# Projections as three fp16 products, values copied by ScalarE, rows normalised by GpSimd, in an attention and experts kernel

## The reference

```
x = x + attention(layernorm(x))      # 16 heads of 16, causal; qkv = xn @ W_qkv + b_qkv; out @ W_out + b_out
x = x + experts(layernorm(x))        # 8 experts, top 2 per token, h = gelu(xn @ w1 + b1), out = h @ w2 + b2
```

## Time and profile before

| | |
|---|---|
| median of 3 runs | 950.83 us (948.45 to 956.42) |
| the profiled execution | 945.29 us, span of its records 943.5 us |
| mean granted TensorE clock | 0.931 of 2.4 GHz |
| busy: PE, DVE, ACT, POOL | 89%, 74%, 61%, 49% |
| chain that ended last, by engine | PE 52%, DVE 17%, DMA 14%, SPq 7%, issue 4% |

### The profile page before, as it was taken

How to read it: one execution, slowest core, us unless ns; L and a number is a source line. 1 busy time by engine, 2 the same in 40 slices (tenths; PEclk the granted TensorE clock), 3 DMA queues, 4 the chain that set the end, 5 groups by cost and what they waited for, 6 DMA issues and landing times.

```text
span 943.5 us, 21008 instructions
## 1 busy us (share of the span) xinstructions
PE 835.8 (89%) x6760; PEld 553.9 (59%) x6760; DVE 697.6 (74%) x1566; ACT 572.8 (61%) x1048; POOL 465.0 (49%) x575
## 2 busy tenths in 40 slices
PE   4899987877888979888898699998999999999996
PEld 3555422332243525333343589887888888888875
DVE  6777888868659798898986487884686766566664
ACT  2777466656758787877978374563544554455453
POOL 4200032323535665757486647784567564555441
PEclk9999988888887888889897899999999999999999
DMA  9888767754666868567855965445535554544341
GB/s 208 269 278 263 247 179 231 208 143 145 192 182 189 202 169 215 152 195 188 210 118 146 251 115 110 75 85 99 80 53 100 81 77 63 87 77 78 58 70 24
DMA packets 185047, 139.40 MB, mean 148 GB/s; under 512 B 98064, under 2 KB 167568, under 8 KB 184816
## 3 DMA queue, kind: packets, MB, share of 16 engines
q1 hardware_dynamic: 153444, 95.16, 39.7%
q0 software_dynamic: 15776, 18.95, 13.1%
q10 hardware_dynamic: 15724, 23.95, 7.9%
HBM read 83.63 MB, written 44.80 MB: 136 GB/s over the span
## 4 chain that ended last, share of the span: by engine, by line
PE 52%; DVE 17%; DMA 14%; SPq 7%; issue 4%; POOL 2%; ACT 1%; POOLq 0%; ACTq 0%; DVEq 0%
PE banks L777 17%; PE banks L795 17%; PE banks L599 5%; DVE arena L1240 3%; PE banks L716 3%; DMA arena<-inverse_sums 2%; DMA weighed_values<-arena 2%; SPq L1818 2%; PE banks L702 2%; DVE weights L1402 2%; PE banks L589 2%; SPq L1816 2%; DVE arena L1242 2%; DMA arena<-token_rows,arena 2%; DVE arena L1237 2%
## 5 line engine op out<-in xcount | busy, mean ns | idle before, releaser
L996 ACT ACTIVATE arena<-banks,arena 128x256 f32<-128x256 f32 (+1 forms) x312 | 152.8, 542 | 187.1 <-PE banks L777 96.2
L777 PE MATMUL banks<-arena,weights 128*128 128x256 f16 (+1 forms) x1872 | 205.3, 266 | 12.3 <-DMA arena<-arena 11.7
L777 PEld LDWEIGHTS banks<-arena,weights 128*128 x1872 | 174.7, 98 | 38.0 <-issue 14.4
L795 PE MATMUL banks<-weights,arena 128*128 x1704 | 193.8, 273 | 0.8 <-DVE arena L1532 0.8
L1739 POOL DMA_INDIRECT out<-arena x71 | 116.0, 1634 | 141.4 <-DVE arena L1543 89.8
L795 PEld LDWEIGHTS banks<-weights,arena 128*128 128x128 f16 x1704 | 165.2, 98 | 22.3 <-issue 1.7
L658 PE MATMUL banks<-arena 64*128 64x128 f16 (+3 forms) x512 | 121.4, 334 | 19.4 <-ACT arena L907 6.9
L1530 DVE TENSOR_SCALAR arena<-arena 128x512 f16<-128x512 f32 (+1 forms) x156 | 75.3, 483 | 74.8 <-ACT arena L996 73.2
L630 PE MATMUL banks<-arena 62*128 62x384 f16 (+3 forms) x512 | 95.7, 330 | 34.3 <-DVE arena L1237 11.6
L1532 DVE SCALAR_TENSOR_TENSOR arena<-arena 128x512 f16<-128x512 f32 (+1 forms) x156 | 110.1, 706 | 5.5
L658 PEld LDWEIGHTS banks<-arena 64*128 64x128 f16 x512 | 38.4, 100 | 105.4 <-issue 34.4
(11 more groups left out here) (199 smaller groups left out, 1283.1 us busy)
## 6 DMA issues: line engine op xcount, KB each, us to landing
weights<-in_L_ffn_w ACTq DMA_DIRECT2D x16, 1024.0 KB, 8.3
arena<-in_L_ffn_w SPq DMA_DIRECT2D x32, 512.0 KB, 4.9
qk_parts<-weights SPq DMA_DIRECT2D x64, 128.0 KB
arena<-qk_parts SPq DMA_DIRECT2D x128, 64.0 KB, 3.5
weighed_values<-arena SPq DMA_DIRECT2D x32, 256.0 KB
token_rows<-arena SPq DMA_DIRECT2D x12, 512.0 KB, 4.2
arena<-qk_parts SPq DMA_DIRECT2D x128, 32.0 KB, 3.7
arena<-weighed_values SPq DMA_DIRECT2D x32, 128.0 KB
```

The lines of the kernel that those rows point to most:

```text
L777: m = pe.matmul(bank[:, c * TILE:c * TILE + WIDTH[j]], w1[:, k, wp, f:f + P], xp[:, k, 0:WIDTH[j]], start=(i == 0), stop=(i == len(terms) ...
L795: m = pe.matmul(bank[:, c * D:(c + 1) * D], hp[:, f, c * P:(c + 1) * P], w2[:, f // (FC // 2), wp, f % (FC // 2), :], start=(f == 0 and i ...
L996: m = act.activation(h_32[r % 2][:, c, 0:WIDTH[j]], banks[:, 1 + c2, c * TILE:c * TILE + WIDTH[j]], ACT.Gelu, bias=b1_now[j % 2][:, 2 * c2 ...
```

## The change

- **TensorE.** Batch 0 stays in fp32. In batches 1 to 7 each fp32 product becomes three fp16 products (high by high, high by low, low by high) of parts of the rows and of the weights. The order within a batch becomes values 0, c = 0, values 1, c = 1, transposes, c = 2, c = 3. After batch 1 two small products make `b_v @ W_out` (`value_bias`).
- **ScalarE.** The transposed rows are copied as an fp16 part, scaled by 16; the values are copied here (`copy_v`), without a bias; the full fp32 copies of query and key go for batches 1 to 7. It makes the fp16 part of W_qkv once (three instructions of 512 columns) and no longer normalises batches 2 to 7.
- **VectorE.** It makes the low parts of the rows (two per batch, `low_rows`) and of W_qkv (three once) and those of query and key straight from PSUM. The bias of the values is added to the output bias once. `know_rows` takes single batches from batch 3 on, and eight of its small steps are replaced by one power on GpSimd, for which it waits. `qk_scales_2` comes ahead of `know_rows(1)`. Magnitudes: one matrix in each of batches 2, 3, 4 and 6; two matrices more are left to attention, where loads and magnitudes stand 30 ticks apart rather than 36.
- **GpSimd.** The roots (`row_roots`), the columns of W_v in another order (two copies), the memset of `rows`, and the normalising of batches 2 to 7 (four instructions of 256 columns each). The split of the output bias comes in batch 2.
- **SyncE.** b1 goes to tick 132 of attention, the eleven DMAs of the empty rows to ticks 60 to 260, the search for the expert scales and the first weight splits some 12 to 18 ticks later.

```diff
-            at(i * 36 + 30, "load_weights", i + EARLY)
-            at(i * 36 + 92, "magnitude", (i + EARLY, 0))
-            at(i * 36 + 110, "magnitude", (i + EARLY, 1))
+            at(i * 30 + 30, "load_weights", i + EARLY)
+            at(i * 30 + 92, "magnitude", (i + EARLY, 0))
+            at(i * 30 + 110, "magnitude", (i + EARLY, 1))
...
+        for i in range(B - PARTS[0][0] + 2):
+            at(60 + 40 * i, "spare", i)
+        at(132, "b1", 0)
+        at(384, "find_scales", 0)
...
-        together = [[0]] + [list(range(b, min(b + 2, B))) for b in range(1, B, 2)]
+        together = [[0], [1, 2]] + [[b] for b in range(3, B)]
...
+                    w.wait_ge(sem("w_in_low"), 1)
+                    w.wait_ge(sem("x_low"), 2 * b)
+                    terms = [(k, w_in[:, wp], x_parts[b % 2][:, xp]) for k in range(KC)
+                             for xp, wp in ((0, 0), (0, 1), (1, 0))]
...
-                for half in range(2):
-                    for s in range(2):
-                        tt = half * 2 + s
-                        for k in range(KC):
-                            m = pe.matmul(banks[:, (4, 7)[half], s * D:(s + 1) * D],
-                                          x_T[b % 2][:, k, tt * P:(tt + 1) * P], w_qkv[:, k, 2 * D:3 * D],
-                                          start=(k == 0), stop=(k == KC - 1))
...
+                    if c < 2:
+                        for s in range(2):
+                            tt = c * 2 + s
+                            for i, (k, w_, x_) in enumerate(terms):
+                                m = pe.matmul(banks[:, (4, 7)[c], s * D:(s + 1) * D], x_[:, k, tt * P:(tt + 1) * P],
+                                              w_v[:, k, :] if b == 0 else w_[:, k, 2 * D:3 * D], start=(i == 0), stop=(i == last))
+                        m.then_inc(sem("v_made"), 1)
                     number = 2 * KC * b + c
                     bank = banks[:, 5 + c % 2, :]
                     if number >= 2:
-                        w.wait_ge(sem("qk_full"), number - 1)
-                    for k in range(KC):
-                        m = pe.matmul(bank, w_qkv[:, k, c * P:(c + 1) * P], x_T[b % 2][:, k, :],
-                                      start=(k == 0), stop=(k == KC - 1))
+                        w.wait_ge(sem("qk_low"), number - 1)
+                    for i, (k, w_, x_) in enumerate(terms):
+                        m = pe.matmul(bank, w_[:, k, c * P:(c + 1) * P], x_[:, k, :], start=(i == 0), stop=(i == last))
                     m.then_inc(sem("qk_made"), 1)
...
+            def value_bias():
+
+                w.wait_ge(sem("vectors_in"), 80)
+                for k in range(KC):
+                    m = pe.matmul(banks[:, 3, 0:D], b_v[:, k:k + 1].broadcast_to([P, P]), w_out[:, k, :],
+                                  start=(k == 0), stop=(k == KC - 1))
+                m.then_inc(sem("value_bias"), 1)
...
+                    else:
+
+                        act.activation(qk_part[b % 2][c][:, 0, :], banks[:, 5 + c % 2, :], ACT.Identity,
+                                       bias=b_qk[:, c:c + 1], scale=1.0).then_inc(sem("qk_high"), 1)
...
+                w.wait_ge(sem("roots_known"), i + 1)
+                for step in range(2, 5):
                     m = own.mark(rsqrt_step(step, variance_, inverse, rest))
                     yield
...
+            def low_rows(b):
+                for k in range(KC):
+                    w.wait_ge(sem("xT"), 2 * b + k + 1)
+                    v.scalar_tensor_tensor(x_parts[b % 2][:, 1, k, :], banks[:, (4, 7)[k], :], ROWS_UP,
+                                           x_parts[b % 2][:, 0, k, :], ALU.mult, ALU.subtract).then_inc(sem("x_low"), 1)
...
+                    else:
+                        w.wait_ge(sem("qk_high"), number - 2 * KC + 1)
+                        v.scalar_tensor_tensor(low, banks[:, 5 + c % 2, :], b_qk[:, c:c + 1], qk_part[b % 2][c][:, 0, :],
+                                               ALU.add, ALU.subtract).then_inc(sem("qk_low"), 1)
+                    if c == 1 and b + 1 < B:
+                        low_rows(b + 1)
                     if b >= OPEN and opening[2 * KC * (b - OPEN) + c]:
                         maxima(*opening[2 * KC * (b - OPEN) + c])
-                    w.wait_ge(sem("qk_full"), number + 1)
-                    both(qk_part[b % 2][c][:, 1, :], qk_full[number % 2], qk_part[b % 2][c][:, 0, :], ALU.subtract).then_inc(
-                        sem("qk_low"), 1)
+                    for _ in range(4):
+                        next(following, None)
+                    if c % 2 == 1 and b in MAGNITUDES_IN:
+                        magnitude(MAGNITUDES_IN.index(b), (c // 2,))
...
+            qk_scales_2()
             for _ in know_rows(1):
...
+            def row_roots(i):
+                n = TT * len(together[i])
+                w.wait_ge(sem("sums_known"), i + 1)
+                g.tensor_tensor(newton_1[i % 2][1][:, 0:n], newton_1[i % 2][0][:, 0:n],
+                                minus_half.rearrange("p n t -> p (n t)")[:, 0:n], ALU.pow).then_inc(sem("roots_known"), 1)
+
+            row_roots(0)
+            w.wait_ge(sem("w_qkv_in"), 32)
+            for k in range(KC):
+                g.tensor_copy(w_v[:, k, :].rearrange("p (g d h) -> p g h d", g=NG, h=HG),
+                              w_qkv[:, k, 2 * D:3 * D].rearrange("p (g h d) -> p g h d", g=NG, h=HG)).then_inc(
+                    sem("w_v_turned"), 1)
             w.wait_ge(sem("qk_own"), 1)
             g.partition_all_reduce(Q_ALL, Q_OWN, P, bass.bass_isa.ReduceOp.max).then_inc(sem("qk_all"), 1)
             g.memset(v_blocks[1][:, :, HG * HD:V_WIDE], 1.0)
             for s in range(4):
                 g.memset(q_st[s], 0.0)
                 m = g.memset(k_st[s], float(2 ** SHIFT))
+                if s == 1:
+                    row_roots(1)
...
+            def normalise(b):
+                i = group_of[b]
+                col = TT * together[i].index(b)
+                w.wait_ge(sem("rows_known"), i + 1)
+                w.wait_ge(sem("normed"), b)
+                w.wait_ge(sem("x_turned"), 2 * (b - 2) + 2)
+                for tt in range(TT):
+                    m = g.tensor_scalar(x_norm[b % 2][:, tt, :], x_in[b % 4][:, tt, :],
+                                        newton_1[i % 2][1][:, col + tt:col + tt + 1],
+                                        newton_1[i % 2][3][:, col + tt:col + tt + 1], ALU.mult, ALU.add)
+                m.then_inc(sem("normed"), 1)
...
+            for b in range(1, B):
+                if b + 1 < B:
+                    normalise(b + 1)
+                if b + 2 < B:
+                    row_roots(group_of[b + 2])
+                if b == 2:
+                    split_bias()
+                if b == B - 2:
+                    top_split(0)
...
-            for b in range(PARTS[0][0], B):
-                sp.dma_start(rows_dram[b * T:(b + 1) * T, 0:D].rearrange("(t p) d -> p t d", p=P), rows).then_inc(
-                    sem("spare_rows"), 16)
-                sp.dma_start(rows_dram[b * T:(b + 1) * T, D:ROW].rearrange("(t p) e -> p t e", p=P),
-                             rows[:, :, 0:E]).then_inc(sem("spare_rows"), 16)
...
+                elif stage == "spare":
+                    lay_spare(n)
+                elif stage == "b1":
+                    sp.dma_start(b1_sb, t["L0_ffn_b1"].rearrange("e (c p) -> p e c", p=P),
+                                 allow_slow_non_contiguous=True).then_inc(sem("b1_in"), 16)
```

224 lines of the change are left out of this document (137 added, 87 removed).

## The result

The changed kernel took **960.49 us** (median of 9 runs, 957.56 to 966.66) against 950.83 us (9 runs of the kernel before beside it, 939.97 to 966.98). The ratio is **1.0141, 95% interval 1.0106 to 1.0175**: slower. The forecast was 949 us with 936 to 963, and its likeliest case, no change, did not come; the rival of 962 us came nearest. The profiled execution took 960.49 us, its span 958.6 us.

A forecast was written before the change was run, and what follows sets the result against it. TensorE was taken to bound the projections and VectorE early attention. Projections -14.5, start +7.2 and attention +5.2 summed to -2.1 us; with the 5.5 us offset of the median carried over, 949 us, range 936 to 963.

The forecast's parts named there:

- the rival of 962 us: Early attention: SyncE stands behind b1's load up to 15.4 us instead of 2, giving 962 us; chance 0.15.
- four signs: Wrong if: first fp16 product before 32 us, batches near 9, SyncE issue over 5 near unit 6, projections clock below 0.95.
- The products: TensorE in the projections: fp16 products take a batch from 11.2 to 8.8 us, 2.4 us less.
- The pace of VectorE: Projections: VectorE needs 10.0 us in batches 2 to 4, above TensorE's 8.8; seven batches 73.8 us, 14.5 us gained.
- The start: Before batch 1: its fp16 products start at 38.0 us where they were at 30.78, 7.2 us lost.
- two changes of code: GpSimd at the start: changing code before the reduction and before the power of 8 columns, up to 7.3 us each.
- The first rival: Start: GpSimd's changes of code are off the path, batch 1 at 28.3 to 31 us, 939 to 942 us; chance 0.23.
- Attention: Early attention: magnitudes 2.2 us, b1 2 us and empty rows 1 us, together about 5 us lost.
- SyncE stands behind b1: Attention, tick 132: b1's 2.20 + 13.19 us recur, shifting the load of unit 6 and later ones; 962 us, chance 0.15.
- the third rival: TensorE's clock falls to a mean of 0.86 through waits at the start and in each batch; 955 us, chance 0.12.
- The empty rows: SyncE in attention: two issues of 0.43 us at five places, mostly in gaps, cost 1 us (bounds 0 and 9).
- The magnitudes: VectorE in attention: two matrices more, four magnitudes of 1.12 us, half counted, 2.2 us lost (bounds 0 and 4.8).

The follow-up runs named there:

- bias_split_late: The changed kernel with the split of the output bias on GpSimd in batch 6 in place of batch 2; 959.91 us, ratio 1.0139 to the kernel before.
- b1_back: The changed kernel with only the load of b1 back at the start of SyncE's queue; 950.01 us, ratio 0.9976 to the kernel before.
- reduction_first: The changed kernel with roots of batches 0 to 2 on VectorE and GpSimd's reduction ahead of its two copies; 977.25 us, ratio 1.0062 to the kernel before.
- roots_on_vector: The changed kernel with roots of batches 0 to 2 back on VectorE in eleven small steps; 963.77 us, ratio 1.0106 to the kernel before.

## Why the prediction was wrong

**What bounds the kernel: right.** TensorE was the bound of the projections, and work moved into attention met another bound. But I read attention's bound as VectorE's busy share alone. The queue that feeds both engines was in the account only for b1 and the empty rows, at 3 us in all. Three of the four signs that I had named for being wrong came: batches near 9 us, a SyncE issue of over 5 us near the load of unit 6, and a granted clock below 0.95 in the projections.

**The products: right. The pace of VectorE: too slow.** 12 fp16 products of 256 columns and 6 of 512 take about 1.3 us, as the 1.32 that I took; `low` and `low_rows` came near the 0.65 us taken. Batches 2 and 4 took 8.67 us each, which is TensorE's 8.8; I had put 10.1 on the strength of VectorE's 10.0, and VectorE was busy for only 6.2 and 7.0 us of them. Batch 3 took 15.0 us for 10.1, with the 3.85 us of batch 4's late rows and 1.7 us more for the twelve products behind them. Batches 1 to 7 took from 38.91 to 115.3 us, 76.4 us against 73.8, so that the sum is near in part because these two misses have opposite signs. GpSimd's normalising was counted at nothing with the sentence that the transposes would wait if it were late; the split of the output bias and its three DMA issues, 59.70 to 64.69 us, stood right ahead of it and were not put into that sum.

**The start: both idles came, the size in part by luck.** Forecast 38.0, measured 38.91. The sum has two changes of code at 7.3 us each. No run shows that GpSimd changes its code there; the traces have idles of 6.73 and 7.00 us that nothing in the profile ends, at the two places. ScalarE had batch 1 normalised at 31.88 us, 1.1 ahead of the sum. From there I had put 5.0 us and it took 7.0: TensorE had waited 7.49 us, the granted clock was 0.62 from 33.50 to 38.50 us, and eight fp32 products, 3.60 us in the kernel before at 1.00, took 5.37:

```profile
33.70 5.37 PE L623 MATMUL banks<-weights 128*128 128x512 f32 x8
```

The place given for the idle of the reduction was too narrow: it also came with only the two copies ahead, at 8.41 us, and not where the reduction stands first, behind its wait for VectorE (7.49 us). That before it was hidden in such a wait, as the sum has it, no trace shows. And the sum had no memset that holds VectorE (in the kernel before one tensor_scalar was held for 1.24 us at 17.61, a row that I had passed over); in the changed kernel that hold hid behind the second idle, and it took its price only when the powers were gone. The first rival, with this time off the path and batch 1 at 28.3 to 31 us, did not come true.

**Attention: this step failed.** "I take 2 us on the path: issue within the gap, part of the rest on the load (bounds 0 and 15.4)". The issue did fill the gap, with 2.45 us, and then nothing of the gap was left (0.1 us): the next issue stood for 10.37 us, and with b1 back at the start units 1 and 2 were 8.3 us closer, unit 2 came 10.6 us earlier, and the ratio fell by 0.0165, some 16 us with wide bounds. The rival SyncE stands behind b1 had the place, the mechanism and the time, 962 us against 960.49, and I gave it 0.15. Against it I had put that other loads filled the engines at the start; in attention they were nearly as full: the DMA share was 1.16 from 9.19 to 22.38 us in the kernel before, and 1.09 from 147.50 to 158.00 us in the changed one. The rows at hand give a sum of that size: the load that waits has no slack but SyncE's gap of 4.2 us, and 2.20 + 13.19 less that gap is 11.2. But this is no proof of a rule: in the kernel before, where that gap was read, b1 alone stopped SyncE for 2.69 and 1.84 us and cost 0.0031.

**The empty rows: probably too low.** 1 us taken, bounds 0 and 9; measured 4.0 to 6.6 us at unit 2, and 0.0042 in ratio, not clear of zero. I counted issues of 0.43 us and not the bytes that stand ahead of the next load. **The magnitudes: too high**, 2.2 us taken, 0.9983 (0.9949 to 1.0017) measured. **Not in the sum at all:** that unit 3's load is issued behind the stores of batch 7, so that the first us won in the projections turn into a wait (4.64 us at 127.11).

**The clock.** Besides the start, it was granted at 0.90 and 0.93 from 60 to 80 us, around and behind the wait of 3.85 us, as the third rival had it, and at 1.00 in batches 1, 2 and 4 to 7. In the start's stretches it was 0.50 from 28.00 to 33.50 us and 1.00 from 38.50 on; eight transposes took 1.97 us at 0.50 (31.94) and 1.04 at 1.00 (44.12). The 0.62 from 33.50 to 38.50 us is a mean between these two levels. By bias_split_late the second dip cost nothing at the end.

So it is shown by runs that the loss comes from b1's place in SyncE's queue and from the order at the start: either one mended brings the kernel back to the time of the one before. How the loss is shared between them is not shown, since their prices overlap. For the empty rows alone the ratio shows nothing beyond its interval. Open are why the lead over the kernel before shrinks again between units 23 and 31 in most of these traces (from -6.6 to +1.9 us in b1_back), and what the later splits cost.

## What to carry to other kernels

Price a DMA that is moved by what stands in its queue behind it, and by how long that can wait: behind b1's 8192 runs of one word the next issue stood for 2.69 us with 3.9 us free ahead of it, and for 10.37 with 0.1. Such a transfer belongs where nothing is queued. At the start b1's load cost 0.0165 less in ratio than in attention, and in the kernel before 0.0031 less, not clear of zero. Before costing an engine's idle time at nothing, ask what its next instruction shuts out: order GpSimd's memsets behind the small steps of VectorE that others wait for (8.89 us against 0.65 for one of them), and put an instruction that stood behind an idle with no releaser first, behind a wait that is there anyway (GpSimd's reduction at 11.44 us against 16.83). When a stage gets faster, look at who issues the first load of the next stage.

## What the hardware did that was not expected

- A VectorE tensor_scalar of three columns (eight in the kernel before) beside a run of GpSimd memsets of 128x1024 lasted until the whole run ended: 8.89 us in reduction_first, 8.08 in roots_on_vector, 3.62 in the changed kernel and 1.24 in the kernel before, to 21.20, 25.53, 20.31 and 18.85 us, each within 0.02 us of the last memset's end. With the memsets held back the same instruction took 0.65 us and ended with GpSimd's two copies (12.93 and 12.91 us); its like take 0.17. scalar_tensor_tensor (0.16 us at 16.50 in the changed kernel) and the statistics (0.35 us each at 15.49 in the kernel before, 0.34 in the changed kernel at 21.50 with no memset beside them) took their usual times beside such memsets.
- 32 KB in runs of one word held the next issue of the same queue for 10.37 us right behind them, and for 2.69 and later 1.84 us where the next issue came 3.9 us after.
- GpSimd stood idle, with nothing in the profile to wait for, ahead of the reduction for 6.73 us behind a power and two copies and for 8.41 us behind two copies alone (roots_on_vector), and for 7.00 us ahead of the power of eight columns behind memsets. With the reduction first it followed its wait for VectorE, 7.49 us in reduction_first, without such an idle.
